# Order of the multiply-accumulates on VectorE in a DLRM tower: from two tiles by turns to tile by tile, with waits per tile

## The reference

```python
x0 = prev = e                                   # (b, 32 fields, 32 dims)
for W in (filter_0, filter_1):
    z = einsum('bhd,bmd->bhmd', x0, prev)       # all products of two fields, per dimension
    cur = relu(einsum('bpd,pn->bnd', z.reshape(b, h*m, d), W[0]))   # 128 outputs
    prev = cur
z = sum over d of concat(cur_1, cur_2)          # (512, 256)
h = concat(z, dense_ctx)                        # (512, 272)
y = relu(relu(h @ W_top1 + b1) @ W_top2 + b2) @ W_top3
```

## Time and profile before

| | |
|---|---|
| median of 3 runs | 908.58 us (907.87 to 910.68) |
| the profiled execution | 908.48 us, its span 906.7 us |
| PE, DVE, ACT, POOL busy | 93%, 82%, 80%, 79% |
| MACs on DVE (L765) | 2048, mean 342 ns |
| scaled copies on ACT (L563) | 2048, mean 382 ns |
| matmuls of layer 2 on PE (L871, L877) | 3072 |
| mean granted TensorE clock | 0.996 |

### The profile page before, as it was taken

One profiled execution on the slowest core, in us unless ns is written; L12 is line 12 of the kernel. 1 busy time (PEld: TensorE's weight loads), 2 busy tenths in 40 slices (PEclk: granted clock), 3 DMA queues, 4 the chain that ended last, 5 costly groups with the idle time before them and its releaser, 6 DMA issues.

```text
span 906.7 us, 18108 instructions
## 1 busy us (share of the span) xinstructions
PE 846.9 (93%) x3607; PEld 668.3 (74%) x3607; DVE 748.0 (82%) x2363; ACT 726.2 (80%) x2418; POOL 716.1 (79%) x739
## 2 busy tenths in 40 slices
PE   0189999999998999999999999999999999999997
PEld 0167777777786777787777777787777777787873
DVE  4158888898886889888888898888888998888893
ACT  2158888988886898988888888888888898888882
POOL 7777899878887889878888989877777766677761
PEclk9999999999999999999999999999999999999999
DMA  7035676666765666666577565766676665655440
GB/s 191 12 91 134 156 171 150 145 141 136 158 146 142 147 146 149 136 150 146 144 166 165 141 155 114 156 145 142 161 166 144 143 147 127 155 139 144 94 93 1
DMA packets 59774, 124.41 MB, mean 137 GB/s; under 512 B 9377, under 2 KB 18145, under 8 KB 59746
## 3 DMA queue, kind: packets, MB, share of 16 engines
q0 software_dynamic: 22240, 68.17, 40.2%
q1 hardware_dynamic: 37506, 55.96, 19.7%
HBM read 54.99 MB, written 3.05 MB: 64 GB/s over the span
## 4 chain that ended last, share of the span: by engine, by line
PE 60%; DVE 13%; POOL 12%; issue 11%; DMA 1%; ACT 1%; DVEq 1%; SPq 0%; POOLq 0%; ACTq 0%
PE bank L871 49%; DVE acc L765 10%; PE bank L809 9%; POOL rows L344 4%; POOL pair_low L382 2%; POOL half L364 2%; POOL rows_next L397 1%; POOL parts L356 1%; DVE pair L629 1%; PE bank L918 1%; POOL w_sb L366 1%; DVE parts L765 1%; DVE cur_low L640 1%; DMA shifts<-x_scratch 1%; ACT parts L563 0%
## 5 line engine op out<-in xcount | busy, mean ns | idle before, releaser
L563 ACT ACTIVATE parts<-bank,x 128x128 f32<-128x128 f32 x2048 | 591.6, 382 | 118.0 <-PE bank L871 108.6
L765 DVE SCALAR_TENSOR_TENSOR acc<-bank,x,acc 128x128 f32<-128x128 f32 x1792 | 485.3, 342 | 94.2 <-PE bank L871 94.1
L871 PE MATMUL bank<-w_high,cur_high 128*128 128x512 f32 x1024 | 407.5, 398 | 5.7 <-DVE acc L765 3.6
L871 PE MATMUL bank<-w_low,cur_high 128*128 128x512 f32 x1024 | 400.1, 391 | 0.0
L871 PE MATMUL bank<-w_high,cur_low 128*128 128x512 f32 x992 | 388.6, 392 | 0.0
L871 PEld LDWEIGHTS bank<-w_high,cur_high 128*128 128x128 f32 x1024 | 192.5, 188 | 62.3 <-DVE acc L765 19.1
L871 PEld LDWEIGHTS bank<-w_low,cur_high 128*128 128x128 f32 x1024 | 192.6, 188 | 39.4
L871 PEld LDWEIGHTS bank<-w_high,cur_low 128*128 128x128 f32 x992 | 186.5, 188 | 41.2
L364 POOL TENSOR_TENSOR half<-parts 128x512 f32<-128x512 f32 x126 | 165.1, 1310 | 61.5 <-DMA parts<-parts 61.3
L382 POOL TENSOR_TENSOR pair_low<-pair,pair_high 128x512 fp32r<-128x512 f32 x124 | 158.6, 1300 | 28.0 <-ACT pair_high L498 24.0
L397 POOL DMA_INDIRECT rows_next<-table_dram,ids_next x96 | 98.1, 1022 | 30.6 <-issue 30.3
(11 more groups left out here) (90 smaller groups left out, 492.1 us busy)
## 6 DMA issues: line engine op xcount, KB each, us to landing
parts<-parts POOLq DMA_DIRECT2D x126, 512.0 KB, 5.7
shifts<-x_scratch SPq DMA_DIRECT2D x155, 256.0 KB, 3.9
x<-x_scratch SPq DMA_DIRECT2D x31, 256.0 KB, 2.9
x_scratch<-turned SPq DMA_DIRECT2D x31, 64.0 KB
rows_next<-table_dram,ids_next POOLq DMA_INDIRECT x96
wt<-w_top_dram SPq DMA_DIRECT2D x2, 512.0 KB
x_scratch<-turned SPq DMA_DIRECT2D x31, 32.0 KB
rows<-table_dram,ids_sb POOLq DMA_INDIRECT x32, 2.4
```

The lines of the kernel that those rows point to most:

```text
L563: ins = nc.scalar.activation(parts[q][ab][:, at:at + N2], act_bank[ab][:, i * N2:(i + 1) * N2], ACT.Copy, scale=x0[u][:, h, 2 * q + ab:2 * ...
L765: nc.vector.scalar_tensor_tensor(out=dst, in0=dve_bank[e % 2 * 2 + ab][:, i * N2:(i + 1) * N2], scalar=x0[u][:, h, 2 * q + ab:2 * q + ab + ...
L871: return nc.tensor.matmul(dst[:], cur_half[u][:, cols], w1_half[:, fields], **flags)
```

## The change

The pair product of step 4 moves from DVE's slot 12 to slot 16 and its cast from ACT's slot 16 to 17. On POOL the subtraction of step 4 moves behind `add_halves`, and those of steps 1 and 2 move ahead of the gathers. On DVE a slot is now tile a's four MACs in a row and then tile b's. Before each four DVE waits for that tile alone. A MAC that isn't its tile's first in the slot waits for the one right in front; the first one waits for the last one of the same tile in slot e - 1. PE waits, before it fills a DVE bank, for the four MACs of that tile in slot e - 2.

```diff
-DVE_PAIR = {0: (1,), 4: (2, 0), 8: (3,), 12: (4,)}
+DVE_PAIR = {0: (1,), 4: (2, 0), 8: (3,), 16: (4,)}
-ACT_PAIR_HIGH = {4: 1, 8: 2, 13: 3, 16: 4}
+ACT_PAIR_HIGH = {4: 1, 8: 2, 13: 3, 17: 4}
...
                     if t % DC == 0 and (next_block or t < tiles - DC):
-                        pair_lows(k * CPB + t // DC + 1, (2, 3))
+                        pair_lows(k * CPB + t // DC + 1, (2,))
                     add_halves(k * (tiles // 2) + t // 2, t // 2 % 2)
+                    if t % DC == 0 and (next_block or t < tiles - DC):
+                        pair_lows(k * CPB + t // DC + 1, (3,))
+                    if t % DC == 2 and (next_block or t < tiles - DC - 2):
+                        pair_lows(k * CPB + t // DC + 2, (0, 1))
                     for s in (t, t + 1):
                         if (next_block and s < rows_at) or (one_after and s > rows_at):
                             for f in late[s]:
                                 gather(f)
-                    if t % DC == 2 and (next_block or t < tiles - DC - 2):
-                        pair_lows(k * CPB + t // DC + 2, (0, 1))
...
-                            dve.wait_ge(for_dve, (pair_no * EACH + e + 1) * 2)
-
-                            for n in range(e * HG, (e + 1) * HG):
-                                for ab in range(2):
+                            for ab in range(2):
+                                dve.wait_ge(for_dve, (pair_no * EACH + e) * 2 + ab + 1)
+                                for n in range(e * HG, (e + 1) * HG):
...
                                         dve.wait_ge(act_prod, pair_no * (2 * EACH) + ab + 1)
+                                    elif i > 0:
+                                        dve.wait_ge(mac, pair_no * (2 * MACS) + (2 * e + ab) * HG + i)
                                     else:
-                                        dve.wait_ge(mac, pair_no * (2 * MACS) + 2 * n + ab - 1)
+                                        dve.wait_ge(mac, pair_no * (2 * MACS) + (2 * e + ab - 1) * HG)
...
-                                    wait(pe, mac, (pair_no * EACH + e - 1) * (2 * HG))
+                                    wait(pe, mac, ((pair_no * EACH + e - 2) * 2 + ab + 1) * HG)
```

## The result

The changed kernel takes 1006.88 us (median of 4 runs, 1004.77 to 1009.91) against 908.74 us: a ratio of 1.108, 95% interval 1.105 to 1.111. The profiled execution took 1004.77 us, its span 1002.9. DVE has become the engine that sets the pace.

The account below looks back on a forecast made before the run. PE sets the pace before, DVE after: 5.66 us per chunk for MACs waiting on the one in front, less DVE's absorbed waits for PE, adds 81.4 us to 908.5, giving 990 us; 8 in 10 range 965 to 1035.

Parts of the forecast that it names:

- The MACs in a row: DVE's MACs that wait for the one right in front: 0.118 us more each, 48 per chunk, 5.66 us per chunk.
- rival 1: On DVE's MACs: the wait on the predecessor is free or nearly so, PE remains the bound, 886 to 908 us; chance 0.07.
- Its size: DVE's MAC step: 0.342 us plus a gap of 0.034, so 0.376; 0.258 between tiles; chunks of 28.28 us.
- the signs: Expected in the profile: MACs 0.37 to 0.38 us apart, PE's waits for MACs 80 to 90 us, DVE near 95% busy.
- DVE's slack: DVE's waits for PE at slots 20 and 24: about 2.8 us per chunk free; rival 1's threshold used 2.97 us.
- The waits per tile: DVE's and PE's waits on single tiles: worth nothing but robustness where DVE sets the pace; extra wait entry cost 0.
- The orders: Step 4's later pair and POOL's subtractions ahead of the gathers: hidden work, cost 0.
- the argument given for the late step 4: POOL subtracts behind add_halves; the chain reaches cur_high at T + 7.5, DVE asks at T + 9.5: hidden, 2.0 us to spare.
- the gathers have until the next block: On POOL, subtractions of steps 1 and 2 delay gathers by 2.55 us in every second pair of tiles; cost 0.

Follow-up runs that it names:

- its first experiment: The kernel before with one edit, each MAC waiting for the one right in front, tiles still by turns: 1046.4 us, ratio 1.151.
- the best kernel: Changed kernel with two accumulators per tile, both changes of order undone, and step 0's pair product moved from DVE's slot 4 to 8: 893.15 us, ratio 0.982.

## Why the prediction was right, and where it was off

**The MACs in a row.** Right, and the whole of the loss. The wait alone makes the kernel before slower by 137 us; without it the same order of MACs, with the old orders around it, runs at 903 us. So rival 1 falls. The rule that it leaned on, in the Trainium skill, "VectorE: DVE Perf Modes", section "The DRAIN you can't avoid", is that a semaphore after each operation costs nothing extra; it doesn't hold for these waits: the step is 0.26 us with one instruction between and 0.38 with none, in the same order of the same instructions (the kernel before, and its first experiment).

**Its size.** Forecast 0.376 us, from L684 behind L681; the timeline gives 0.384 on the average. The gap behind the end is the 0.034 forecast, but the records themselves grew, from a mean of 342 to 349 ns (351 for a MAC that waits for the one in front). And I kept 0.258 for the step between tiles, which is 0.268, because the record in front is the longer one. That is some 48 x 0.008 + 16 x 0.010 = 0.54 us per chunk too little. Against it stand small waits that I left in and DVE no longer has, such as the one for `turned` (3.1 us in all); I did not add them up. The undisturbed chunks take 28.3 and 28.7, on the average 28.5 in place of 28.28, 7 us over the span. Two of the signs were off too. PE's waits for MACs came to 65 us and not 80 to 90, while 44 us (38.8 and 4.8) went to waits for `pair_hl`, which no term had. DVE is 88% busy and not near 95%: the gaps between records, 1536 of 0.034 us, count as idle, some 52 us.

**The clock.** It stood in no term. Eight chunks were 0.9 us longer, 7 us in the profiled execution; the run with extra matmuls got 5.4 us back. With the chunks' 7 us it puts the last chunk's start at 951.8, not at 938.8. The last chunk takes 28.6 us, not 27.7, and the tail 0.9 us more: together this carries 990 to 1005, the profiled execution. That the median of the runs is 2 us more was not traced further.

**DVE's slack.** "About 2.8 us per chunk is all that DVE can take on for nothing" was right as a sum for a DVE that becomes the bound, which is why the forecast held. As a threshold, which rival 1 used, it was wrong: 2.0 us per chunk already cost 27 us. Idle time at slots 20 and 24 paid for 26 of the 65 us added all over the chunk.

**The waits per tile.** "Worth nothing but robustness" was wrong: they are worth 17 us here. At slots 20 and 24, behind the product groups, PE is late with tile b, and DVE starts on tile a without it; my sentence "if PE were late, it would hold tile b alone" had the case, and I priced it at nothing. I had argued from DVE's never waiting, which is what these waits bring about. How much of the 17 us is DVE's wait and how much the earlier release of the banks stays open.

**The orders.** "Cost 0" holds for the changed kernel (1006.3 without them), and by the argument given for the late step 4 (908.7 alone). For the gathers the step failed: "the gathers have until the next block" looked at who needs the gathers and not at what POOL did in their place. It stands waiting for casts, and the sums and the next subtractions queue behind. On a kernel with PE as the bound this costs 36 us. That it cost nothing in the changed kernel was luck: the wait in front had made DVE's chunk longer than the 27.6 us that the orders force.

## What to carry to other kernels

An accumulation chain on VectorE wants one independent instruction between two links: by turns over two tiles, or over two accumulators of one tile; for instructions this short (longer ones weren't measured), waiting for the one right in front costs nearly half of the instruction's step again. Idle time of an engine, summed over a cycle, is not slack for work at any place of the cycle, and a reordering in an in-order queue is judged by what the queue would otherwise have done while it waits. Undo the parts of a change one by one even when the forecast holds: here one part was worth 17 us, another would have cost 36 on its own, and the best kernel keeps two of four, the order tile by tile (with two accumulators) and the waits per tile. What each of these two is worth there was not run.

## What the runs showed of the hardware

- A VectorE scalar_tensor_tensor of 128x128 from PSUM starts 0.26 us behind the one in front, and 0.38 us if it waits for that one's semaphore: 0.035 us behind the end of its record, where it started 0.083 us ahead of it without the wait. Its own record then takes 0.351 us and not 0.342.
- In the changed kernel, whose PE stalls for up to 1.3 us at one place of each chunk, the granted clock fell to 1.2 GHz for eight short spells in the loops; in the kernel with one more matmul per slot it stayed at 2.4 GHz there, and the time fell by 5.4 us. That kernel's weight loads waited 6.8 us for MACs and not 50.7; the stalls of up to 1.3 us for `pair_hl` were still there.
- The kernel with waits per slot has more of PE's waits for MACs (107.6 us of weight loads and 55.8 of matmuls, against 50.7 and 14.7), hardly any for `pair_hl` (0.6 us), and a mean granted clock of 0.998: more waiting for MACs alone did not bring the clock down. What does was not settled.
